# One of GpSimd's two tap products moved to VectorE, diagonal weights of the images moved to GpSimd, base product issued last

## What is computed

```python
pooled = x.mean((2, 3))
hdn = _ln(pooled @ w_fc1.T, ln1_w, ln1_b, axis=-1)
dyn_w = (hdn @ w_fc2.T).reshape(b * c, 1, K, K)              # K = 5: 25 weights for each image and channel
out = lax.conv_general_dilated(x.reshape(1, b * c, h, w), dyn_w, ..., feature_group_count=b * c)
u = out.mean(1, keepdims=True)                               # over the channels
s2 = jnp.square(out - u).mean(1, keepdims=True)
out = (out - u) * lax.rsqrt(s2 + EPS)
out = ln2_w * out + ln2_b
out = jax.nn.gelu(jnp.einsum('bchw,oc->bohw', out, w_expand), approximate=False)
gx = jnp.sqrt(jnp.sum(jnp.square(out), axis=(2, 3), keepdims=True))
nx = gx / (gx.mean(1, keepdims=True) + EPS)
out = g * (out * nx) + bt + out
return jnp.einsum('bohw,co->bchw', out, w_shrink) + x
```

## Time and profile before

| | |
|---|---|
| median of 3 runs | 917.48 us (916.5 to 917.58) |
| the profiled execution | 917.29 us, span 915.6 us |
| busy share of the span | PE 90%, DVE 68%, ACT 46%, POOL 62% |
| block one | to about 503 us |
| block two | from there to the end; GpSimd's last instruction ends at 869.4 us |
| GpSimd in block two | 43.2 of 44.5 us busy in the stretch from 694.5 to 739 us, VectorE 36.4, ScalarE 35.2, TensorE 39.9 |
| mean granted clock of TensorE | 0.96 of full speed over the span and in that stretch |

### The profile page before, as it was taken

One profiled execution on the slowest core, in us unless ns is written; L12 is line 12 of the kernel. 1 busy time (PEld: TensorE's weight loads), 2 busy tenths in 40 slices (PEclk: granted clock), 3 DMA queues, 4 the chain that ended last, 5 costly groups with the idle time before them and its releaser, 6 DMA issues. The chain is left out here.

```text
span 915.6 us, 16129 instructions
## 1 busy us (share of the span) xinstructions
PE 824.0 (90%) x5639; PEld 674.4 (74%) x5639; DVE 620.2 (68%) x1125; ACT 419.1 (46%) x504; POOL 566.8 (62%) x477
## 2 busy tenths in 40 slices
PE   5999999999999999999998667789898989898775
PEld 5999999999999999999998544445454544445331
DVE  4666666666666666688888387577878787876622
ACT  4680006777730000000000345788787878786752
POOL 2333333333333333388888399999999999999900
PEclk9999999999999999999999687899999999999989
DMA  7750000000000000000000100000222222222113
GB/s 136 173 129 0 0 0 2 0 0 0 0 1 0 0 0 0 1 1 0 0 0 0 45 23 22 23 23 23 46 46 45 46 46 46 46 55 60 24 38 78
DMA packets 51190, 27.00 MB, mean 29 GB/s; under 512 B 40720, under 2 KB 49104, under 8 KB 51152
## 3 DMA queue, kind: packets, MB, share of 16 engines
q1 hardware_dynamic: 51152, 26.51, 13.0%
HBM read 9.98 MB, written 8.39 MB: 20 GB/s over the span
## 5 line engine op out<-in xcount | busy, mean ns | idle before, releaser
L490 PE MATMUL psum<-line_hi,taps_hi 128*128 128x256 f32 x1270 | 203.0, 292 | 12.1 <-DVE taps_lo L386 8.9
L504 PE MATMUL psum<-line_lo,taps_hi 128*128 128x256 f32 x1270 | 202.7, 291 | 0.8 <-DVE line_lo L439 0.8
L498 PE MATMUL psum<-line_hi,taps_lo 128*128 128x256 f32 x1270 | 202.5, 291 | 0.0
L439 DVE SCALAR_TENSOR_TENSOR line_lo<-psum,rest 128x256 fp32r<-128x256 f32 x254 | 108.1, 426 | 124.3 <-POOL rest L266 115.7
L266 POOL TENSOR_TENSOR rest<-x,line_hi 128x256 f32<-128x256 f32 x127 | 83.0, 654 | 169.3 <-DVE line_hi L430 169.3
L490 PEld LDWEIGHTS psum<-line_hi,taps_hi 128*128 128x128 f32 x1270 | 177.1, 192 | 13.3 <-issue 9.7
L504 PEld LDWEIGHTS psum<-line_lo,taps_hi 128*128 128x128 f32 x1270 | 176.8, 192 | 1.9 <-DVE line_lo L439 1.7
L498 PEld LDWEIGHTS psum<-line_hi,taps_lo 128*128 128x128 f32 x1270 | 177.1, 192 | 0.0
L266 POOL TENSOR_TENSOR rest<-by_h,line_hi 128x256 f32<-128x256 f32 x127 | 91.8, 722 | 83.4 <-DVE line_hi L430 83.4
L318 ACT ACTIVATE by_h<-x (+1 forms) x128 | 85.6, 669 | 106.3 <-DVE x L419 104.7
L714 POOL TENSOR_TENSOR part<-part,prod 128x960 f32<-128x960 f32 (+2 forms) x48 | 113.4, 2362 | 18.5 <-issue 13.9
(11 more groups left out here) (129 smaller groups left out, 1052.8 us busy)
## 6 DMA issues: line engine op xcount, KB each, us to landing
stage<-in_x_dram SPq DMA_DIRECT2D x32, 256.0 KB, 4.2
out_dram<-x SPq DMA_DIRECT2D x32, 256.0 KB, 4.3
crossed<-x SPq DMA_DIRECT2D x16, 256.0 KB, 3.6
crossed<-x SPq DMA_DIRECT2D x16, 240.0 KB, 3.7
fc_in<-in_L_conv_w_fc_dram SPq DMA_DIRECT2D x2, 100.0 KB
taps<-in_L_conv_k_td_dram SPq DMA_DIRECT2D x2, 80.0 KB, 3.5
taps<-in_L_conv_k_dt_dram SPq DMA_DIRECT2D x2, 80.0 KB, 3.6
taps<-in_L_conv_k_lr_dram SPq DMA_DIRECT2D x2, 80.0 KB, 3.8
```

The source lines that it names most:

```text
L439: dve.scalar_tensor_tensor(out=line_lo[:, (slot + 1) % SLOTS, :, part], in0=as_lines(line_ps[slot][:, 0:LINE]), scalar=0.0, in1=as_lines(r ...
L490: mm = pe.matmul(line_ps[slot][:, 0:LINE], taps_hi[:, s, d, :], line_hi[:, slot, :, d:d + WP], start=(d == 0), stop=(d == OFFSETS - 1))
L498: pe.matmul(line_ps[slot][:, 0:LINE], taps_lo[:, s, d, :], line_hi[:, slot, :, d:d + WP], start=False, stop=False, skip_group_check=True)
L504: mm = pe.matmul(line_ps[slot][:, 0:LINE], taps_hi[:, s, d, :], line_lo[:, slot, :, d:d + WP], start=False, stop=(d == OFFSETS - 1), skip_ ...
```

## The change

`POOL_TAPS` keeps ("up", 3); ("down", 3) becomes a tap of VectorE, the tenth. The remaining own product of GpSimd is made ahead of the adds of ScalarE's products (`own_product`) and added behind them (`add_own`). `make_dyn` moves from VectorE to GpSimd for images 1 to 7, into the even units behind `split_low`; that of image 0 stays on VectorE. ScalarE issues products 1, 2, 3 and then the base; GpSimd's adds wait for all four. Three small buffers share memory differently.

```diff
--- before.py
+++ after.py
@@ -56,10 +56,11 @@
 
 PE_TAPS = [(1, s) for s in range(K)]
 DVE_TAPS = [("cross", 0), ("cross", 1), ("cross", 3), ("cross", 4), ("up", 0), ("up", 4), ("down", 0), ("down", 4),
-            ("cross", 2)]
+            ("down", 3), ("cross", 2)]
 MIDDLE = [("down", 2), ("up", 2)]
-ACT_TAPS = [MIDDLE + [("up", 1), ("down", 1)], MIDDLE[::-1] + [("up", 1), ("down", 1)]]
-POOL_TAPS = [("up", 3), ("down", 3)]
+SIDES = [("up", 1), ("down", 1)]
+POOL_TAPS = [("up", 3)]
+ACT_TAPS = [MIDDLE + SIDES, MIDDLE[::-1] + SIDES]
 
 
 def build(nc, x, k_td, k_dt, k_lr, k_rl, fc1, ln1_w, ln1_b, fc2, ln2_w, ln2_b,
...
@@ -715,16 +714,21 @@
 
             def add_product(u, n):
                 _, rows, cols, _ = place(u, *ACT_TAPS[u % 2][n])
-                pool.wait_ge(prod_ready, N_ACT * u + n + 1)
-                pool.wait_ge(part_step, PART_STEPS * u + n - 1)
+                pool.wait_ge(prod_ready, N_ACT * (u + 1))
+                if u + n > 1:
+                    pool.wait_ge(part_step, PART_STEPS * u + n - 1)
                 add_part(u, rows, cols, prod[:, n - 1, rows, cols])
 
-            def own_tap(u, n):
-                src, rows, cols, weight = place(u, *POOL_TAPS[n])
-                step = PART_STEPS * u + N_ACT - 1 + n
-                pool.wait_ge(part_step, step)
-                pool.tensor_scalar(own[:, rows, cols], src, weight, None, ALU.mult).then_inc(own_step, 1)
-                pool.wait_ge(own_step, N_POOL * u + n + 1)
+            def own_product(u, i):
+                src, rows, cols, weight = place(u, *POOL_TAPS[i])
+                if u + i > 0:
+                    pool.wait_ge(part_step, PART_STEPS * u + (N_ACT - 1 + i if i else 0))
+                pool.tensor_scalar(own[:, rows, cols], src, weight, None, ALU.mult).then_inc(own_made, 1)
+
+            def add_own(u, i):
+                _, rows, cols, _ = place(u, *POOL_TAPS[i])
+                pool.wait_ge(own_made, N_OWN * u + i + 1)
+                pool.wait_ge(part_step, PART_STEPS * u + N_ACT - 1 + i)
                 add_part(u, rows, cols, own[:, rows, cols])
 
             def add_inner(u):
@@ -733,14 +737,28 @@
                 dst = inner[:, u % INNERS, :, :]
                 pool.tensor_tensor(dst, dst, part[:, u % 2, :, :], ALU.add).then_inc(inner_ready, 1)
 
+            def make_dyn(b):
+                shape = [P, 2 * len(PE_TAPS), C]
+                diagonal = kept["ident_half"][:, :].rearrange("p (a c) -> p a c", a=1).to_broadcast(shape)
+                if b >= 2:
+                    pool.wait_ge(conv_done, 4 * (b - 1))
+                for t, full in ((tap_hi, dyn_hi), (tap_lo, dyn_lo)):
+                    t = t[:, b, :, :].bitcast(F32).rearrange("p t (o a) -> p (t o) a", a=1).to_broadcast(shape)
+                    last = pool.tensor_tensor(full[:, b % 2, :, :, :].rearrange("p t o c -> p (t o) c"),
+                                              diagonal, t, ALU.mult)
+                last.then_inc(dyn_ready, 1)
+
             pool.wait_ge(taps_known, 1)
+            pool.wait_ge(dyn_ready, 1)
             for u in range(UNITS):
+                own_product(u, 0)
                 for n in range(1, N_ACT):
                     add_product(u, n)
+                add_own(u, 0)
                 if u + 2 < UNITS:
                     split_low(u + 2)
-                for n in range(N_POOL):
-                    own_tap(u, n)
+                if u % 2 == 0 and u // 2 + 1 < B:
+                    make_dyn(u // 2 + 1)
                 add_inner(u)
 
         @block.scalar
@@ -754,7 +772,7 @@
             def product(u, n):
                 src, rows, cols, weight = place(u, *ACT_TAPS[u % 2][n])
                 if n == 0:
-                    if u >= 2:
+                    if u > 1:
                         act.wait_ge(inner_ready, u - 1)
                     dst = part[:, u % 2, rows, cols]
                 else:
@@ -826,7 +844,7 @@
                 def products(lo, hi):
                     if s + 1 < UNITS:
                         for n in range(lo, min(hi, N_ACT)):
-                            product(s + 1, n)
+                            product(s + 1, (n + 1) % N_ACT)
 
                 if 2 <= s + 2 < UNITS:
                     split_high(s + 2)
@@ -860,14 +878,12 @@
                 dve.tensor_tensor(x_lo[:, u, :, 2:2 + W], x[:, 0, ROWS * u:ROWS * (u + 1), :],
                                   x_hi[:, u, :, 2:2 + W].bitcast(F32), ALU.subtract).then_inc(xlo_first, 1)
 
-            def make_dyn(b):
+            def make_dyn():
                 shape = [P, 2 * len(PE_TAPS), C]
                 diagonal = kept["ident_half"][:, :].rearrange("p (a c) -> p a c", a=1).to_broadcast(shape)
-                if b >= 2:
-                    dve.wait_ge(conv_done, 4 * (b - 1))
                 for t, full in ((tap_hi, dyn_hi), (tap_lo, dyn_lo)):
-                    t = t[:, b, :, :].bitcast(F32).rearrange("p t (o a) -> p (t o) a", a=1).to_broadcast(shape)
-                    last = dve.tensor_tensor(full[:, b % 2, :, :, :].rearrange("p t o c -> p (t o) c"),
+                    t = t[:, 0, :, :].bitcast(F32).rearrange("p t (o a) -> p (t o) a", a=1).to_broadcast(shape)
+                    last = dve.tensor_tensor(full[:, 0, :, :, :].rearrange("p t o c -> p (t o) c"),
                                              diagonal, t, ALU.mult)
                 last.then_inc(dyn_ready, 1)
 
@@ -975,7 +991,7 @@
             link(last)
             link(dve.tensor_copy(tap_hi[:, :, :, :], tap[:, :, :, :]))
             link(dve.tensor_tensor(tap_lo[:, :, :, :], tap[:, :, :, :], tap_hi[:, :, :, :].bitcast(F32), ALU.subtract))
-            make_dyn(0)
+            make_dyn()
             dve.tensor_copy(tap_cross[0:C, :, :], tap_all[0:C, K:2 * K, :])
             link(dve.tensor_copy(tap_cross[C:P, :, :], tap_all[C:P, 3 * K:4 * K, :]))
             dve.sem_inc(taps_known, 1)
@@ -995,14 +1011,12 @@
                 take(1)
                 if v >= 0:
                     finish(v, 0)
-                take(1)
+                take(2)
                 if e in range(UNITS):
                     norm(e, 1)
                 take(2)
                 if v >= 0:
                     finish(v, 1)
-                if s % 2 == 0 and (s + 2) // 2 < B:
-                    make_dyn((s + 2) // 2)
                 if 0 < e <= UNITS and e % 2 == 0:
                     sum_energy(e // 2 - 1)
                 take(2)
```

More of the change, by code:

```diff
@@ L84, in build @@
             ln1_wb=sb("ln1_wb", [B, 2, CR]),
+            fc2_t=sb("fc2_t", [P, T_GROUPS, P]),
             own_t=sb("own_t", [P, T_GROUP]),
@@ L92, in build @@
         )
-        at = -(-nc.sbuf_base // 32) * 32
-        sb("slab", [P, ROWS * W + 8])
-        kept["fc2_t"] = nc.alloc_sbuf_tensor_at("fc2_t", [P, T_GROUPS, P], F32, offset=at)
-        kept["own"] = nc.alloc_sbuf_tensor_at("own", [P, ROWS, W], F32, offset=at)
         scans(nc, bank, kept, x, (k_td, k_dt, k_lr, k_rl), fc1, ln1_w, ln1_b, fc2, ln2_w, ln2_b,
@@ L564, in sem @@
             return ctx.enter_context(nc.semaphore(name))
-        N_DVE, N_ACT, N_POOL = len(DVE_TAPS), len(ACT_TAPS[0]), len(POOL_TAPS)
-        PART_STEPS = N_ACT - 1 + N_POOL
+        N_DVE, N_ACT = len(DVE_TAPS), len(ACT_TAPS[0])
+        N_OWN = len(POOL_TAPS)
+        PART_STEPS = N_ACT - 1 + N_OWN
         VAR_STEPS = 2
@@ L578, in block_two @@
         prod = sb("prod", [P, N_ACT - 1, ROWS, W])
-        own = kept["own"]
+        own = sb("own", [P, ROWS, W])
         part = sb("part", [P, 2, ROWS, W])
@@ L597, in block_two @@
         hid = sb("hid", [B, 3, CR])
-        hid_each = sb("hid_each", [B, T_GROUP, CR])
+        hid_each = squares[0:B, 0:T_GROUP * CR].rearrange("b (t r) -> b t r", t=T_GROUP)
         hid_stat = sb("hid_stat", [B, 4])
-        hid_own = sb("hid_own", [P, T_GROUP, B])
+        hid_own = squares[:, 256:256 + T_GROUP * B].rearrange("p (t b) -> p t b", t=T_GROUP)
         tap_all = sb("tap_all", [P, K * K, B])
```

2 lines of the change are left out of this document (1 added, 1 removed).

## The result

The changed kernel takes 924.31 us (median of 4 executions, 924.04 to 928.83) against 917.45 us for the kernel before in the same comparison: a ratio of 1.0085, interval 1.0056 to 1.0113. It is slower by 0.9%; the interval lies above 1, so this is a real loss, though a small one.

What follows compares the result with a forecast made beforehand. GpSimd bounded the kernel before, at 21.92 us a unit; the way round all engines would bound it after. Turns summed to inner(14) at 847.7 and 918.9 us warm; 8.2 for 11 cold turns gave 927.1, range 914 to 934.

Steps and rivals of the forecast that it cites:

- GpSimd's own time no longer matters: GpSimd's queue needs 16.6 us, or 19.6 with two diagonal products, of the 21.9 or 22.7 between starts of inner.
- warm turn: One inner start to the next with TensorE at full clock: 21.9 us in odd units, 22.7 in even ones with response.
- the pair: Two diagonal products on GpSimd in 7 of 16 units, 1.5 us each, 3 an image; hidden up to 6.1 us.
- The ring: Way round all engines from inner through adds, ScalarE's products, gelus, var and last tap to next inner: 21.9 or 22.7 us.
- The extra tap and the removed pair on VectorE: VectorE gains a tap, about 1.25 us, and loses the diagonals; the tap costs nothing in turns 1 to 14.
- The ends: inner(0) at 538.8 against 540.3; var(15) 11.1 us after inner(14), at 858.8 against 857.25, with everything behind it hanging on it.
- The warm ring: Rival, chance 0.18: TensorE's hole is there but its clock seldom falls; 919 us, from 915 to 922.
- TensorE's clock: Low clock after TensorE's pause costs 0.7 to 0.8 us more a turn; 11 of 13 turns taken as cold, 8.2 us.
- The hole: TensorE has nothing to do until the second gelu is done: 2.4 us, in odd turns 3.4 us.
- The signs named in advance: ScalarE's product waits 3 to 4 us, GpSimd 2 to 5; inner to inner 22 to 24; low clock in most turns.
- GpSimd keeps the pace, about 870: Rival, chance 0.08: product 1 does not wait last, a unit takes 18.1 to 19 us; about 870 us.
- Worse ring, 937: Rival, chance 0.09: low clock through fourth expand and statistics, or diagonals over 6.1 us; 1.3 us more a turn, about 937.

Runs made afterwards that it cites:

- the filler: The changed kernel plus sixteen useless TensorE products repeating the spreading of rstd ahead of the third expand, only in slots with convolution work: 918.68 us, ratio 1.002.
- both orders as before: The changed kernel with GpSimd's own product moved back behind the three adds and ScalarE's base product issued first again: 876.08 us, ratio 0.9565.
- the filler in every slot: The changed kernel plus the same sixteen useless TensorE products ahead of the third expand, also in the last slots without convolution work: 925.04 us, ratio 1.0091.
- two of my own edits: Each against the changed kernel: own product between first and second add, 935.63 us; one TensorE convolution piece moved ahead of the third expand, 941.52 us.

## Why the prediction was right, point by point

**GpSimd's own time no longer matters: right.** It was put at 16.6 us in odd units; with the filler, in warm turn 7, GpSimd idles 5.37 of 21.98 us, so its queue takes 16.6. The diagonal products, estimated at 1.5 us each, took 1.27, against 0.82 on an undisturbed VectorE. GpSimd idles 3.96 us in the even turn above: the pair is hidden, as said.

**The ring: right, nearly to the tenth.**

| in a turn, us | predicted | measured |
|---|---|---|
| product 1, from the start of inner, even / odd | 7.25 / 7.4 | 7.24 / 7.38 |
| var, even / odd | 16.5 / 16.8 | 16.60 / 16.82 (odd with the filler) |
| warm turn, even / odd | 22.7 / 21.9 | 22.76 / 22.0 (odd with the filler) |
| turn 1 | 19.7 | 19.61 |
| turn 2, turn 4 | 21.6, 22.7 (warm) | 22.55, 23.45 (with the filler, fourth expand cold) |

That it is this ring, and which of its links count, is shown by the experiments: taking own product out of it gives 41 us, taking the second gelu out from behind product 1 gives 35, and moving own product between the adds leaves var where it was in a warm turn. Turns 2 and 4 are 0.95 and 0.75 us longer than said even with the filler. The clock accounts for most of it: with the fourth expand cold, var comes 17.3 us into both turns, 0.7 us later than in warm even turns.

**The extra tap and the removed pair on VectorE: right in turns 1 to 14.** VectorE idles 5.75 us ahead of var in turn 8, more than the 4.00 of before. inner(0) started at 537.67, 1.1 us earlier than said, since block two's first tap was at 524.70 against 526.10.

**The ends: the way to var(15) right, the rest decided by the clock.** var(15) came 11.0 us after inner(14), said was 11.1. From there to the end I had carried over the 58.35 us of before. It was 58.1 us in the profiled execution of the change and 56.4 in the one with the filler, although both run the same instructions there. TensorE behind rstd in turn 15, first the change, then the kernel with the filler:

```profile
871.76 2.08 PE L1104 MATMUL psum<-rstd,spread 128*128 128x128 f32 x8 [3.10 <-DVE rstd L918]
...
862.88 1.16 PE L1104 MATMUL psum<-rstd,spread 128*128 128x128 f32 x8 [3.10 <-DVE rstd L918]
```

The pause is the same, 3.10 us, and only one of the two is followed by the low clock. In the profiled executions of all kernels but one (the filler in every slot, 61.4) this last part takes 56.4 to 59.7 us. So differences of 2 or 3 us between two kernels here can be the clock of the last part alone.

The warm ring was predicted at 918.9, and the kernel with the filler took 918.7. That is so close by luck. In its profiled execution (918.33) the start was 1.0 us early, the turns up to inner(14) were 2.4 us too long and the part behind it 2.1 us too short.

**TensorE's clock: right in kind, the term mis-sized.** The hole ends where it was said, 9.5 us into the turn. In even turns from the sixth on TensorE idles 2.21 to 2.25 us ahead of the third expand, and every expand there is warm (1.13 us). In odd turns from the fifth on it is 2.70 or 2.71 us, not the 3.4 said, and each of them has a cold expand. The 3.4 was mis-sized because I moved the second expand with the first gelu: the gelu is 0.73 us earlier than in even turns (2.04 against 2.77 us into the turn), but the expand behind it, which also stands behind the spreading of rstd, only 0.32 (3.92 against 4.24). I had taken 11 of 13 turns as cold at 0.75 us each, 8.2 us. In the profiled execution seven turns are longer than those with the filler, all six odd ones and turn 4, by 0.7 to 2.0 us each, 9.1 in all; in the medians the term is 5.6. The count was too high, the price of one too low. I had read it from a turn of before where one expand was cold, and 0.7 us is what turns 7 and 11 cost, with the third expand alone cold (1.71 and 1.69 us). Turns 9 and 13 have both the third and the fourth cold (2.08 and 1.98 us in turn 9) and cost 2.0. Turn 5, with the fourth alone cold, cost 0.85. Why the other three executions are some 4.5 us shorter than the profiled one stays open, since they have no trace; a different count of cold turns, or a different last part, would do it.

The median, 924.3, is 2.8 us below the 927.1 predicted; 2.6 of it is the clock term (5.6 measured for 8.2).

**The signs named in advance.** ScalarE's product waits 3.4 and 4.2 us in a turn (said 3 to 4), GpSimd 5.2 us in the mean for the last tap (2 to 5), inner to inner is 22.5 to 24.7 us in turns 2 to 14 (22 to 24), own product is straight behind inner. All were seen, some a little beyond the range named. The low clock came in 8 of these 13 turns.

**The rivals.** The warm ring isn't what the change does, but it is what the filler makes of it. "GpSimd keeps the pace, about 870" needed product 1 not to wait last; with both orders as before that condition holds, and the time is 876, though TensorE and not GpSimd then sets the pace. "Worse ring, 937" is what two of my own edits ran into (935.6 and 941.5) when they shifted the hole behind the third expand.

## What to carry to other kernels

When the busiest engine is relieved, add up the way round through all engines before you book the gain: for each buffer, from its release to its next filling, with what is queued behind the instruction that waits for it. Here two changes of order, which cost no instruction, decided between 924 and 876 us. A removed wait is worth something only if the next instruction in that queue finds its buffer free.

## What was not expected of the hardware

- The length of a pause of TensorE does not tell what it costs. In the change 2.70 us ahead of the third expand cost 0.7 us in some turns and 2.0 in others, by how long the clock stayed at half, and 2.24 us cost nothing. In the kernel before, pauses of 2.40 to 2.46 us in turns 6, 8, 10, 12 and 14 were followed by expands of 1.89, 1.73, 1.58, 1.42 and 1.27 us. With own product between the adds, 2.85 to 2.88 us ahead of the fourth expand cost nothing in turns 8 and 14, and in turn 10 that expand took 2.08 us.
- Where the pause lies counts as well. The two kernels with it ahead of the fourth expand (2.13 and 3.41 us in the turns shown) are 17 and 11 us slower than the change, since the convolution piece, and in the second the statistics too, is then cold straight ahead of mean_sq.
- Sixteen small repeated products (2.05 us) in the hole kept the granted clock at 1.00 from the fifth turn to the fourteenth and gained 5.6 us. In turns 2 to 4 they ended 2.07 to 2.64 us ahead of the third expand, and the clock still fell in turns 2 and 4. In the last slots, where there is no hole, the kernel that had them there too took 6.4 us more (925.04 against 918.68).
- GpSimd's own product with one input and a weight for each partition is slower than its add of two inputs: 2.66 us against 2.21 for the same 945 elements.
